# Layer 1 of a two-layer graph network: rows carried by transfers, the ELU's and the residual's sums on GpSimd, the maxima over more tiles, the right half of the queries ended first

## What is computed

```
Wh = x1 @ W                                   # (8, 2048, 256)
s_i = Wh @ a[:256];  s_j = Wh @ a[256:]
e = leaky_relu(s_i[:, :, None] + s_j[:, None, :], 0.2)
e = where(adj > 0 or i == j, e, -inf)
h = elu(softmax(e, axis=-1) @ Wh)
out = layernorm(x1 + h)
```

## Time and profile before

| what | us |
|---|---|
| median of 3 runs (lowest, highest) | 3980.1 (3978.75, 3983.96) |
| the profiled execution | 3980.02 |
| its span, first to last instruction | 3978.2 |
| busy in the span: TensorE, VectorE, ScalarE, GpSimd | 3643.7, 3254.2, 2520.5, 2064.1 |
| layer 1's first instruction | 2642.6 |
| layer 1's first and last products (L1324) | 2760.1, 3962.6 |

### The profile page before, as it was taken

One profiled execution on the slowest core, in us unless ns is written; L12 is line 12 of the kernel. 1 busy time (PEld: TensorE's weight loads), 2 busy tenths in 40 slices (PEclk: granted clock), 3 DMA queues, 4 the chain that ended last, 5 costly groups with the idle time before them and its releaser, 6 DMA issues. The chain is left out here.

```text
span 3978.2 us, 135900 instructions
## 1 busy us (share of the span) xinstructions
PE 3643.7 (92%) x57428; PEld 2511.2 (63%) x57428; DVE 3254.2 (82%) x3989; ACT 2520.5 (63%) x3554; POOL 2064.1 (52%) x1068
## 2 busy tenths in 40 slices
PE   6999999999999999999999999942998998999898
PEld 2656756655756655665665675522776777777777
DVE  6786887787788688688788778857989989889897
ACT  3666666666666666666666666622677676776777
POOL 1786787777678687678677768831101011011010
PEclk9999999999999999999999999976999999999999
DMA  6010010010010001001001000042111110110101
GB/s 216 3 37 16 14 40 14 19 35 19 14 40 14 14 19 40 14 14 40 18 15 35 19 14 19 19 164 78 39 43 33 44 54 24 52 54 22 33 28 37
DMA packets 106692, 145.28 MB, mean 37 GB/s; under 512 B 3792, under 2 KB 87632, under 8 KB 104016
## 3 DMA queue, kind: packets, MB, share of 16 engines
q1 hardware_dynamic: 104816, 135.80, 10.2%
q10 hardware_dynamic: 1248, 0.40, 0.1%
HBM read 102.63 MB, written 33.55 MB: 34 GB/s over the span
## 5 line engine op out<-in xcount | busy, mean ns | idle before, releaser
L277 POOL TENSOR_TENSOR psums<-probs 128x1024 f32<-128x1024 f32 x512 | 1288.8, 2517 | 626.7 <-ACT probs L381 624.4
L381 ACT ACTIVATE probs<-probs 128x1024 f32<-128x1024 f32 x1024 | 1083.5, 1058 | 812.8 <-DVE probs L857 791.2
L493 PE MATMUL ctx_ps<-probs,v_rows 64*32 64x512 f32 x16256 | 1477.1, 590 | 11.7 <-DVE seg_ctx L780 10.3
L857 DVE SCALAR_TENSOR_TENSOR probs<-sc_ps,clip_hi 128x1024 f32<-128x1024 f32 x1024 | 1225.0, 1216 | 217.6 <-PE sc_ps L480 206.6
L480 PE MATMUL sc_ps<-q_cols,k_cols 64*32 64x512 f32 x16384 | 1205.0, 592 | 43.9 <-DVE probs L857 43.3
L1324 PE MATMUL out_ps<-wh,e 128*128 128x257 f32 x4096 | 963.7, 388 | 166.0 <-DVE e L1466 157.2
L1324 PEld LDWEIGHTS out_ps<-wh,e 128*128 128x128 f32 x4096 | 777.5, 193 | 326.6 <-DVE e L1466 117.9
L493 PEld LDWEIGHTS ctx_ps<-probs,v_rows 64*32 64x32 f32 x16256 | 664.0, 106 | 289.9 <-issue 190.6
L480 PEld LDWEIGHTS sc_ps<-q_cols,k_cols 64*32 64x32 f32 x16384 | 533.8, 106 | 333.9 <-issue 212.2
L1153 POOL TENSOR_TENSOR rstd<-var_eps,minus_half 128x4 f32<-128x4 f32 x32 | 68.4, 2138 | 1069.6 <-DVE var_eps L1426 1069.6
L487 PE MATMUL den_ps<-psums,ones 64*32 64x512 f32 x4064 | 598.3, 594 | 17.9 <-DVE seg_ctx L780 11.2
(11 more groups left out here) (97 smaller groups left out, 3356.1 us busy)
## 6 DMA issues: line engine op xcount, KB each, us to landing
x_cols<-in_xT SPq DMA_DIRECT2D x8, 2048.0 KB, 7.9
probs<-in_adjT SPq DMA_DIRECT2D x16, 1024.0 KB, 8.4
x_rows<-in_x SPq DMA_DIRECT2D x32, 512.0 KB, 4.1
x<-res SPq DMA_DIRECT2D x32, 512.0 KB, 2.9
x_in<-x SPq DMA_DIRECT2D x8, 2048.0 KB, 10.3
x_res<-x SPq DMA_DIRECT2D x32, 512.0 KB, 4.7
out<-h SPq DMA_DIRECT2D x32, 512.0 KB, 3.2
e<-in_adjT SPq DMA_DIRECT2D x8, 1024.0 KB, 7.8
```

The source lines that it names most:

```text
L277: pool.tensor_tensor(psums[:, q % 2, pair, :], probs[:, (SJ * q) % RING, pair, :], probs[:, (SJ * q + 1) % RING, pair, :], ALU.add).then_i ...
L381: act.activation(probs[:, n % RING, pair, :], probs[:, n % RING, pair, :], ACT.Exp, scale=DH ** -0.5).then_inc(s_exp, 1)
L493: return pe.matmul(ctx_ps[quad(h), z, :], v_rows[head_rows(r), n % JB, at:at + QUAD], probs[head_rows(r), n % RING, h, :], start=start, st ...
L857: dve.scalar_tensor_tensor(out=probs[:, n % RING, pair, :], in0=sc_ps[:, p, :, :], scalar=-LIM, in1=clip_hi[:, j, c * CW:(c + 1) * CW][:, ...
```

## The change

All of it is in layer1.

- s_i becomes a second column beside Wh (wh has F + 3 columns instead of F + 2, column 0 is s_i, column 1 s_j). SP stores that column to DRAM (s_d) and loads it back as 128 partitions x 16 (s_c). The products L1295 and ScalarE's copies of them go.
- The reduced maximum is moved by a transfer from one partition to 128 x 16 (m_c); the four row operations work on 16 columns, all at step 51; SP stores both rows to DRAM (rows_d) and loads each spread over all partitions into best and low, 1 MB each.
- The ELU and the residual become three GpSimd sums of 128x1024: h + neg, x_res + exp, and the sum of both; exp goes to a buffer of its own (e_neg).
- The maxima are at steps 13 + 33 j // 16. Statistics and variance are at step 9, the offset at 10.
- The last two tiles of a chunk are added for the right half first (EARLY = 2), and the reciprocals of the right half wait for that alone (s_right); LATE is 2 instead of 3.

```diff
-    TU, WU, SU = KB * NC, JB, NC
+    TU, WU = KB * NC, JB
+    RJ = N // P
-    uses_at = [1 + u for u in range(TU)] + [10 + 27 * j // JB for j in range(JB)] \
-        + [37 + 2 * c for c in range(NC)]
-    TAKEN = 4
+    uses_at = [1 + u for u in range(TU)] + [9 + 27 * j // JB for j in range(JB)]
+    TAKEN = 3
-    LATE = 3
+    LATE = 2
+    EARLY = 2
-        return 17 + 27 * j // JB
-    ROWS_AT = (53, 55, 57, 59)
+        return 13 + 33 * j // JB
+    INV_AT, STATS_AT, VAR_AT, OFFSET_AT = 2, 9, 9, 10
+    SCALE_AT, EXP_AT, NORM_AT = 2, 4, 13
+    ROWS_AT = 51
...
+            def spread_own(b):
+                sp.wait_ge(s_prepread, count(b, USES, 2 + TU + WU))
+                with nc.allow_non_contiguous_dma(reason="2048 values a batch"):
+                    sp.dma_start(s_d[0].rearrange("(j p) -> p j", p=P), wh[:, b[1] % 2, :, 0]).then_inc(s_sout, 16)
+                sp.wait_ge(s_sout, count(b, 16, 16))
+                sp.dma_start(s_c[:, :], s_d[0].rearrange("(p j) -> p j", p=P)).then_inc(s_sin, 16)
+
+            def make_rows(b):
+                p = b[1] % 2
+                sp.wait_ge(s_all, count(b, 1, 1))
+                sp.dma_start(m_c[:, :], low[0:1, p, :].rearrange("o (q j) -> o q j", j=RJ)).then_inc(s_m, 16)
+                sp.wait_ge(s_rows, count(b, 4, 4))
+                sp.dma_start(rows_d.rearrange("r (p j) -> p r j", p=P), rows_c[:, :, :]).then_inc(s_rout, 16)
+                sp.wait_ge(s_rout, count(b, 16, 16))
+                sp.dma_start(best[:, p, :], rows_d[0].partition_broadcast(P)).then_inc(s_rin, 16)
+                sp.dma_start(low[:, p, :], rows_d[1].partition_broadcast(P)).then_inc(s_rin, 16)
...
                 load_x((0, 1))
+                spread_own((0, 0))
+                make_rows((0, 0))
...
+                    if c == 2 and more:
+                        spread_own(following(b))
+                    if c == NC - 1 and more:
+                        make_rows(following(b))
...
+            def elu_and_residual(b, c):
+                own = h[:, c % 2, :, :]
+                pool.wait_ge(s_min, count(b, NC, c + 1))
+                pool.sem_inc(s_waited, 1)
+                pool.tensor_tensor(own, own, neg[:, :, :], ALU.add).then_inc(s_pos, 1)
+                pool.wait_ge(s_en, count(b, NC, c + 1))
+                pool.wait_ge(s_xr[c % 2], count(b, 16 * (NC // 2), 16 * (c // 2 + 1)))
+                pool.sem_inc(s_waited, 1)
+                pool.tensor_tensor(x_res[:, c % 2, :, :], x_res[:, c % 2, :, :], e_neg[:, :, :], ALU.add)\
+                    .then_inc(s_elu, 1)
+                pool.wait_ge(s_pos, count(b, NC, c + 1))
+                pool.wait_ge(s_elu, count(b, NC, c + 1))
+                pool.sem_inc(s_waited, 1)
+                pool.tensor_tensor(own, own, x_res[:, c % 2, :, :], ALU.add).then_inc(s_r, 1)
...
                     if c == NC - 1 and more:
                         reduce(following(b))
                     if prev:
+                        elu_and_residual(*chunk_before(b, c))
+                    if prev:
                         inverse_deviation(*chunk_before(b, c))
...
                 if n == 0:
-                    act.wait_ge(s_rows, count(b, 4, 4))
+                    act.wait_ge(s_rin, count(b, 32, 32))
...
             order = [(j, (0, 1)) for j in range(LATE)] + [(j, (2, 3)) for j in range(LATE)] \
-                + [(j, range(T)) for j in range(LATE, JB)]
+                + [(j, range(T)) for j in range(LATE, JB - EARLY)] \
+                + [(j, (2, 3)) for j in range(JB - EARLY, JB)] + [(j, (0, 1)) for j in range(JB - EARLY, JB)]
...
             def row_operation(b, k):
...
                 if k == 0:
-                    dve.wait_ge(s_prepread, count(b, USES, 2 + USES))
-                    dve.wait_ge(s_all, count(b, 1, 1))
-
-                    dve.tensor_tensor(low[:, p, :], low[:, p, :], s_row[:, :], ALU.add).then_inc(s_rows, 1)
+                    dve.wait_ge(s_sin, count(b, 16, 16))
+                    dve.wait_ge(s_m, count(b, 16, 16))
+                    dve.tensor_tensor(m_c[:, :], m_c[:, :], s_c[:, :], ALU.add).then_inc(s_rows, 1)
...
             def invert(b, c):
-                dve.wait_ge(s_mm, count(b, STEPS, ERING + (c + 1) * JB))
+                dve.wait_ge(s_right, count(b, NC, c + 1))
                 for t in BANK_ORDER:
+                    if t == 0:
+                        dve.wait_ge(s_mm, count(b, STEPS, ERING + (c + 1) * JB))
                     dve.reciprocal(rden[:, c % 2, t:t + 1], out_ps[:, bank(c, t), F:F + 1]).then_inc(s_rd, 1)
-
-            def elu(b, c):
...
-            def residual(b, c):
...
```

More of the change, by code:

```diff
@@ L930, in _, with layer1 @@
             run(dve, prologue, chunk, tail)
-def layer1(nc, x1, adjT, W, a, out):
+def layer1(nc, x1, adjT, W, a, s_d, rows_d, out):
     B, N, F = x1.shape
@@ L1058, in layer1 @@
         s_rows = sem("rows_made")
+        s_sout = sem("own_terms_stored")
+        s_sin = sem("own_terms_spread")
+        s_m = sem("maxima_spread")
+        s_rout = sem("rows_stored")
+        s_rin = sem("rows_loaded")
         s_hi = sem("high_side_ready")
@@ L1289, in prepare @@
                     for k in range(KB):
-                        last = pe.matmul(prep_ps[:, u % 2, 0:F + 1], x_cols[:, k, j * P:(j + 1) * P],
+                        last = pe.matmul(prep_ps[:, u % 2, 0:F + 2], x_cols[:, k, j * P:(j + 1) * P],
                                          w_ext[:, k, :], start=(k == 0), stop=(k == KB - 1))
-                else:
-                    c = u - TU - WU
-                    for k in range(KB):
-                        last = pe.matmul(prep_ps[:, u % 2, :], wa1_b[:, k, :],
-                                         x_cols[:, k, c * CW:(c + 1) * CW],
-                                         start=(k == 0), stop=(k == KB - 1))
                 last.then_inc(s_prep, 1)
@@ L1324, in steps @@
                             last = pe.matmul(out_ps[:, bank(c, t), 0:F + 1],
-                                             e[:, n % ERING, t * P:(t + 1) * P], wh[:, p, j, 1:F + 2],
+                                             e[:, n % ERING, t * P:(t + 1) * P], wh[:, p, j, 2:F + 3],
                                              start=(j == 0), stop=(j == JB - 1))
-                        if T - 1 in ts:
+                        if j == JB - 1 and T - 1 in ts:
+                            last.then_inc(s_right, 1)
+                        if ts[-1] == (1 if j >= JB - EARLY else T - 1):
                             last.then_inc(s_mm, 1)
@@ L1341, in _ @@
             for k in range(KB):
-                for i, (row, dst) in enumerate(((a1_r, wa1[:, k:k + 1]), (a2_r, w_ext[:, k, 0:1]))):
-                    dve.tensor_tensor_reduce(out=trash[:, 2 * k + i, :], in0=w_ext[:, k, 1:F + 1], in1=row[:, :],
+                for i, (row, dst) in enumerate(((a1_r, w_ext[:, k, 0:1]), (a2_r, w_ext[:, k, 1:2]))):
+                    dve.tensor_tensor_reduce(out=trash[:, 2 * k + i, :], in0=w_ext[:, k, 2:F + 2], in1=row[:, :],
                                              scale=1.0, scalar=0.0, op0=ALU.mult, op1=ALU.add,
                                              accum_out=dst).then_inc(s_wa, 1)
-            dve.wait_ge(s_wa, 2 * KB)
-            dve.wait_ge(s_id, 1)
-            for k in range(KB):
-                dve.tensor_scalar(wa1_b[:, k, :], a1_r[:, 0:P], 0.0, wa1[:, k:k + 1], ALU.mult, ALU.add)\
-                   .then_inc(s_wa, 1)
             def mask_piece(i):
@@ L1446, in prologue @@
                     row_operation((0, 0), k)
-                larger_side((0, 0), 0)
+                for n in range(LARGER_AHEAD):
+                    larger_side((0, 0), n)
             def larger_side(b, n):
@@ L1467, in steps @@
                                                  in1=tile, op0=ALU.max, op1=ALU.min).then_inc(s_e, 1)
-                        if prev and j == 2:
+                        if prev and j == INV_AT:
                             invert(*before)
-                        if prev and j == 6:
-                            elu(*before)
-                        if prev and j == 8:
-                            residual(*before)
-                        if prev and j == 10:
+                        if prev and j == STATS_AT:
                             for t in range(T):
                                 stats(*before, t)
-                        if prev and j == 11:
+                        if prev and j == VAR_AT:
                             variance(*before)
-                        if prev and j == 13:
+                        if prev and j == OFFSET_AT:
                             offset(*before)
@@ L1486, in steps @@
                                 fifths(following(b))
-                            if n in ROWS_AT:
-                                row_operation(following(b), ROWS_AT.index(n))
+                            if n == ROWS_AT:
+                                for k in range(4):
+                                    row_operation(following(b), k)
```

(6 more changed lines are left out.)

78 lines of the change are left out of this document (37 added, 41 removed).

## The result

The changed kernel takes 4026.0 us (median of 4 runs, 4024.8 to 4030.0), the kernel before beside it 3980.6 (3978.8 to 3984.0): a ratio of 1.0115, 95% interval 1.0097 to 1.0132. Slower, as forecast and inside the range, but by 45.4 us where the forecast had 19. The profiled execution has a span of 4023.7 us, 45.5 more than before.

The account below looks back on a forecast made before the run. VectorE's time was taken to set a layer 1 batch, with about 12 us of waits from coupling to TensorE. 3980.0 + 7 (batches) + 8 (lead-in) + 3 (tail) + 1 (last batch) = 3999 us, range 3948 to 4049.

Parts of the forecast that it names:

- the waits that remain: VectorE's waits in a layer 1 batch: 1.8 us for spread maxima, 1.0 power, about 2 coupling, sum 4.8.
- Waits for the maxima: At step 51 of a batch VectorE stands 1.8 us until the reduced, transferred maxima arrive.
- The blocking: Twelve GpSimd sums a batch each stop two-input VectorE work for 2.2 us: 26.4 us a batch.
- stops the next: A GpSimd sum waits for the VectorE instruction in flight, then holds up the following one, 2.2 us each.
- The row transfers: Storing and spread-loading rows: 13.0 + 0.6 us hidden in carrying batches, +8 us in the lead-in.
- Rival (4): Row loads pass their cover by 6 us a batch: 4041 us, 4053 with the lead-in; chance 0.08.
- The new order: Right half early with LATE 2: given nothing in the batches, a gain of 0.7 us in the tail.
- The tail: After the last batch, relu and three GpSimd sums take 8.4 us in place of 4.7; +3 us net.
- The last batch: The batch without preparation of a next one: VectorE 112 us, TensorE 111; +1 us.
- (1): Rival: GpSimd's sums leave VectorE alone, TensorE becomes the bound, a batch is 141 us, 3893 us total; chance 0.10.
- (2): Rival: the block falls where VectorE waited anyway, 153.2 us a batch, 3978 us total; chance 0.17.
- (3): Rival: the block starves TensorE, waits stay 11.6 us, 163.0 a batch, 4047 us total; chance 0.15.

Follow-up runs that it names:

- e3: Kernel after with GpSimd's three sums over only 4 of 1024 columns, the rest of ELU and residual left out: 3885.9 us, ratio 0.976.
- e4: Kernel before plus one GpSimd sum of 4 columns right behind the reduction over partitions, nothing waiting for it: 3978.7 us in one run.
- e7: Kernel before with its ELU and residual as three GpSimd sums a chunk (GpSimd's DMA scratch 2048 bytes, not 4096): 4082.0 us, ratio 1.025.
- e9: Kernel after with the row operations on the spread maxima at step 55 instead of 51, sums left on GpSimd: 4008.7 us, ratio 1.007.
- e10: Kernel after with each GpSimd sum over half of its tile (128x512), the other half left out: 3933.7 us, ratio 0.989.
- e2: Kernel after with only chunk 2's ELU and residual back on VectorE, the other nine sums a batch on GpSimd: 3979.2 us, ratio 0.9997.
- e5: Kernel after with ELU and residual back on VectorE and the row operations at step 55 instead of 51: 3890.8 us, ratio 0.977.
- e1: Kernel after with ELU and residual back on VectorE at steps 6 and 8, all else kept: 3916.3 us, ratio 0.984.
- e6: e1 with the old order of TensorE's halves (LATE 3, EARLY 0, reciprocals behind the whole chunk): 3919.8 us, ratio 0.984.
- e11: e5 with the running maxima back at steps 17 to 42 in place of 13 to 43: 3926.7 us, ratio 0.987.
- e8: Kernel after with the reduction over partitions replaced by an ordinary one-row GpSimd instruction: 4001.6 us, ratio 1.005.

## Why the prediction was right in sign and too small

**The step that failed is "the waits that remain", 4.8 us a batch.** They are 17.6 as the mean over six batches of the kernel after, where the forecast had 1.8 for the spread maxima, 1.0 for the power and 2 of coupling: 7.1 at the statistics, 3.8 for ScalarE, 3.5 for the spread maxima, 2.5 ahead of the reciprocals, 0.7 for the power. The first had no term at all: the forecast let GpSimd start chunk 2's sums when the reduction had ended. The kernel before shows a gap of the same kind ahead of the reduction, 5.86 us of "issue", and the forecast used it there, but it did not ask what the way back costs; the pair of configuration records at each reduction's end, in the kernel before as well, was the sign of it. The way back measured 6.6 to 7.6 us from those records in every run read (after, e3, e4, e7, e9, e10). That the lateness counts, e2 shows; that it counts only with the sums' length behind it, e3. A batch rose by 4.5 us (156.0 to 160.5 as means of six) where +1.0 was forecast, which over seven batches is 24 of the 26 us that the forecast missed.

The Trainium skill, GPSIMD Engine Reference, section "2.1 Instruction dispatch", says that the first call to freshly loaded code costs about 6 us that no instruction of the profile shows. The gap of 5.5 to 6.2 us ahead of each of the kernel after's eight reductions agrees, only that it is not a first call alone that pays it; that the way back is paid too, only the rows say.

**Waits for the maxima**: forecast 1.8 us, measured 3.5, and e5 shows that they cost in full.

**The blocking was sized too high**: 26.4 us a batch forecast, 16 to 17 measured (e1 and e3). A stretched instruction loses 2.2 us as forecast; but not each sum meets one. The first sum of a chunk often falls into a wait of VectorE, and chunk 2's run while VectorE stands at the statistics. The forecast's "stops the next" also failed for the first sums: 18 of the 32 let VectorE begin and end two to five more two-input instructions at full speed, and took 3.7 to 6.5 us for it. So the two errors partly cancel, which is luck: with 126.4 us of VectorE's own (e1's mean batch of 146.7 less its waits of 11.2 and 9.1 of ELU and residual) and the rest of the batch put down to blocking, 126.4 + 16.4 + 17.6 = 160.4, against a forecast of 125.0 + 26.4 + 4.8 = 156.2.

**The row transfers** were forecast as hidden but for the lead-in, +8 there. They were hidden: ScalarE's wait for them is 7.3 us over seven batches in e5. The own terms' store landed in 10.9 us where 7.4 were forecast, and was hidden too. In the lead-in they cost 1.8, because the spread loads took 6.3 us and not the 10.3 of x's load, and the two small transfers ahead of them 2.1 and 1.6, not 2.7 each. Rival (4), late rows, is out.

**The new order** was given nothing: e6 agrees. **The tail**: forecast +3, measured +2.9. **The last batch**: forecast +1, but its four chunks take 116.5 us from TensorE's first product to its last, 29.1 each, where they took 111.8 before, +4.7; the forecast compared the engines' sums of work (112 and 111) and left out that a stop of VectorE is also one of TensorE when both are full.

**The wider spread of the maxima** had no term of its own in the forecast, which took VectorE to set that stretch in any case. e11 gives it 36 us.

**TensorE's work** was forecast at 133.8 us a batch; it was busy 140.5 in the kernel after and 135.4 in e1 (means of six). The granted clock is 0.93 to 0.96 in those batches of the kernel after, 0.97 to 0.99 in the kernel before. It fell behind TensorE's stops: 1.00 in 3045.7 to 3055.7, 0.83 (a mean of its two levels, 2.4 and 1.2 GHz) in each of the three stretches of 10 us up to 3085.7, in which TensorE stood 3.2 us for masks behind the maxima and 4.0 behind the statistics. The forecast had no term for it. e5, at 0.96 in the batch shown, is faster than e1 at 0.99, so the clock is not what orders these runs; what it adds in the kernel after was not separated.

**Rivals.** (1), sums that leave VectorE alone, is out by the 2.85 us masks. Its 3893 us are nearly e5's 3890.8, which has no sums on GpSimd, though with ELU and residual still on VectorE. (2), the block falls on waits anyway, is right for four or five sums of twelve (16.4 us are 7.5 stops of 2.2), and the time doesn't follow since other waits came. (3), 4047, is nearer to the measured 4026 (21 us) than the forecast's own 3999 (27). It saw waits stay at 11.6 and took blocking in full; TensorE's waits for masks, 17.9 us in the batch shown, meet its mark of 15, but part of them stand behind the two new waits: 3.2 us behind the one for the maxima and 4.0 behind the statistics in the batch of the order of time above.

## What to carry to other kernels

Before work moves to an engine that is idle on average, look at what it does just before each moved piece is due: here GpSimd needed some 6 us to get into the reduction over partitions and 7 us to get out, and the piece behind it was on the path. Look for the records of a configuration change: the time runs from them, and they can stand behind a wait, so that idle time ahead of it does not help. Price a sum on GpSimd beside two-input VectorE work at its full length unless VectorE waits there, and weigh it against what the same work costs on VectorE: 9.1 us a batch were exchanged for 16 of standing and 7 of waiting. A change of several parts is worth taking apart: the parts without the sums brought 64 us, and 90 with one step number changed, and the sums hid them.

## What the hardware showed unexpectedly

- Going back from the reduction over partitions to an ordinary GpSimd instruction took 6.6 to 7.6 us from the change of configuration to that instruction's start, in all instances of the kernel after, e3, e4, e7, e9 and e10. It began at the reduction's end or, where the instruction's wait ended later, behind that wait: 4 to 5 us later in e7, 60 us later in the first batch.
- GpSimd can be held off for long by VectorE's two-input instructions in a row: 10.5 us for a sum of four columns in e4, and in the kernel after 3.7 to 6.5 us for 18 of the 32 first sums of a chunk, where one alone takes 2.35. Eight of these 18 are the first instruction behind the reduction, the other ten are not:

```profile
2968.04 6.45 POOL L1206 TENSOR_TENSOR h<-h,neg 128x1024 f32<-128x1024 f32 x1 [22.13 <-ACT neg L1280]
```

  Four instructions of 0.68 us passed it, and the maximum behind them took 4.45 us in place of 2.34. The second and third sums, which follow the one before within 0.2 us, let none pass. What makes the difference was not settled.
- The Trainium skill, SBUF — State Buffer, section "Who interferes with whom", has whoever issues first hold the shared pair for the whole instruction. The second and third sums agree (2.85 us masks beside sums of 2.6 to 2.8). The 18 first sums don't: VectorE's instructions that began after them went ahead of them. Nor does the reduction: of its 7.43 us in the batch shown it held VectorE up for 3.1; instructions of 0.68 ran in its first 1.4 us, and one behind the stretched one while it went on for 2 us more.
- A one-input GpSimd instruction on one partition with 2048 elements took 12.5 us in a batch and 5.35 in the lead-in (e8).
